# Behind the passes of a cross-attention: a reordered last pair of steps, head products in turns, fewer filler products, and one more wait for GpSimd

## What is computed

```python
x = x + xattn(ctx, layernorm(x), ...)     # 16 heads of 64, over 4096 context rows and the 256 rows
x = x + performer(layernorm(x), ...)      # linear attention, 16 heads of 16, 44 features each
x = x + moe(layernorm(x), ...)            # 8 experts, top 2, and a shared one

# the end of xattn, for each head
attn = softmax(sim);  out = attn @ v;  return out @ Wout + bout
# the end of performer
out = (context, qp, d_inv);  h = out @ Wo.T + bo;  return relu(h @ Wfc.T + bfc)
# moe, for each expert e (the shared one is the ninth)
hpre = x @ W1[e] + b1[e];  y = silu(hpre) @ W2[e] + b2[e]
```

## Time and profile before

| | |
|---|---|
| median of 3 runs | 664.42 us (664.26 to 666.61) |
| profiled execution | 664.24 us, of which the span of the trace is 662.5 us |
| PE busy | 649.3 us (98% of the span) |
| DVE, ACT, POOL busy | 508.8, 415.5, 277.0 us |
| granted TensorE clock | 1.0 throughout |
| attention ends, performer ends, last instruction | 514.5, 549.2, 662.5 us |

### The profile page before, as it was taken

The page is one execution under the profiler, slowest core; times in us unless marked ns, Lnnn a source line. Parts: engine busy times, 40 slices in busy tenths (PEclk is TensorE's granted clock), DMA queues, the critical chain, the costliest instruction groups (busy, mean ns, idle before and its releaser), DMA issues. The chain is left out here.

```text
span 662.5 us, 14524 instructions
## 1 busy us (share of the span) xinstructions
PE 649.3 (98%) x5202; PEld 523.5 (79%) x5202; DVE 508.8 (77%) x1010; ACT 415.5 (63%) x881; POOL 277.0 (42%) x210
## 2 busy tenths in 40 slices
PE   8899999999999999999999999999999999899998
PEld 7677777777777777777777777777776878899998
DVE  5899999876877777787777767877776676977674
ACT  5788889866665665665666665656664434655651
POOL 3656556444344354343444434434441300464640
PEclk9999999999999999999999999999999999999999
DMA  6201430010000010000000000000000302665500
GB/s 211 73 34 34 143 132 13 6 33 1 2 17 2 2 49 1 2 1 17 1 1 2 1 1 1 1 17 2 1 1 1 128 1 65 224 216 197 169 21 17
DMA packets 26164, 30.51 MB, mean 46 GB/s; under 512 B 4201, under 2 KB 23794, under 8 KB 26098
## 3 DMA queue, kind: packets, MB, share of 16 engines
q1 hardware_dynamic: 24594, 28.86, 13.2%
q10 hardware_dynamic: 1504, 0.79, 0.4%
HBM read 29.38 MB, written 0.26 MB: 45 GB/s over the span
## 5 line engine op out<-in xcount | busy, mean ns | idle before, releaser
L943 POOL TENSOR_TENSOR k_rms<-k_ss,neg_half 128x4 f32<-128x4 f32 x136 | 195.3, 1436 | 244.9 <-DVE k_ss L797 244.9
L624 ACT ACTIVATE probs<-s_ps,minus_bound 128x512 f32<-128x512 f32 x272 | 165.0, 689 | 103.6 <-PE s_ps L443 101.7
L169 PE MATMUL kv_ps<-w_quad,xn 128*128 128x512 f32 x816 | 206.8, 402 | 0.8 <-DVE xn L744 0.6
L791 DVE SCALAR_TENSOR_TENSOR probs_sum<-probs,tile_mask,probs_sum 128x512 f32<-128x512 f32 x264 | 191.1, 744 | 5.7 <-ACT probs L624 5.6
L169 PEld LDWEIGHTS kv_ps<-w_quad,xn 128*128 128x128 f32 x816 | 147.8, 188 | 39.1 <-DVE xn L744 0.8
L456 PE MATMUL o_ps<-probs,v 128*64 128x256 f32 x1088 | 132.6, 385 | 0.8 <-ACT probs L624 0.7
L443 PEld LDWEIGHTS s_ps<-q_parts,kt 64*128 64x128 f32 x1632 | 101.1, 185 | 26.2 <-issue 24.2
L443 PE MATMUL s_ps<-q_parts,kt 64*128 64x256 f32 x1632 | 114.9, 287 | 0.0
L456 PEld LDWEIGHTS o_ps<-probs,v 128*64 128x64 f32 x1088 | 72.0, 136 | 42.0 <-issue 10.9
L775 DVE SCALAR_TENSOR_TENSOR kn<-k_rms,kv_ps 128x256 f32<-128x256 f32 x136 | 56.4, 414 | 52.0 <-POOL k_rms L943 50.7
L616 ACT ACTIVATE kt<-s_ps 128x256 fp32r<-128x256 f32 x136 | 44.9, 382 | 45.3 <-PE s_ps L427 45.3
(11 more groups left out here) (212 smaller groups left out, 643.7 us busy)
## 6 DMA issues: line engine op xcount, KB each, us to landing
w_raw<-in_ffn_W SPq DMA_DIRECT2D x18, 1024.0 KB, 5.3
rows<-in_ctx SPq DMA_DIRECT2D x7, 512.0 KB, 3.9
w_raw<-in_L_xattn_Wkv SPq DMA_DIRECT2D x6, 256.0 KB, 3.3
wout<-in_L_xattn_Wout SPq DMA_DIRECT2D x4, 256.0 KB, 2.7
wq_raw<-in_L_xattn_Wq SPq DMA_DIRECT2D x3, 256.0 KB, 2.7
rows<-in_ctx SPq DMA_DIRECT2D x2, 256.0 KB, 5.1
w_raw<-in_L_xattn_Wkv ACTq DMA_DIRECT2D x2, 256.0 KB, 5.0
wq_raw<-in_L_xattn_Wq ACTq DMA_DIRECT2D x1, 256.0 KB, 3.9
```

Source lines behind the costliest of these rows:

```text
L169: last = nc.tensor.matmul(out, stationary(k, s), moving(k, m), start=n == 0, stop=n == len(terms) - 1)
L624: nc.scalar.activation(probs[n % P_RING][:, :, c, :], s_ps[n % 2][c][:], ACT.Exp, bias=minus_bound[:]).then_inc(exp_done, 1)
L791: nc.vector.scalar_tensor_tensor(total, probs[n % P_RING][:, :, c, :], seen, total, ALU.mult, ALU.add).then_inc(sum_done, 1)
L943: nc.gpsimd.tensor_tensor(k_rms[n % 2][:].rearrange("p i c -> p (i c)"), k_ss[n % 2][:].rearrange("p i c -> p (i c)"), neg_half[:, 0:4], A ...
```

## The change

Five edits, all behind or at the end of the passes.

1. In turn m = 67, PE makes the scores of steps 134 and 135 ahead of `weight_v(133)` instead of behind it; ACT copies the keys of 134 and 135 ahead of the exponentials of step 133, and DVE splits them ahead of the sums of step 133.
2. The totals and the head products come in turn: totals of pair 0, heads of pair 0, totals of pair 1, heads of pair 1. The totals of a pair get a bank of their own; DVE takes a reciprocal of four for each pair, and adds pair 0 before it waits for pair 1.
3. In the performer, the product with `feat_eps` waits for the first of two subtractions of keys (`k_shifted`) and not for both.
4. The bias products (`bfc`) move ahead of the products with `Wo`, into banks 0 and 7; of the fillers around them, 3 are gone, 3 have become 2, 1 is gone, and the last 3 have become 1.
5. GpSimd waits until VectorE has split both halves of expert 0's activations (`act_lo` at 2) before it enters its loop.

```diff
@@ attention, PE
-            def last_totals():
...
-                for i in range(QT):
-                    for j in range(2):
-                        for c in range(2):
-                            last = nc.tensor.matmul(totals_q[:, i, j, c:c + 1], probs_sum[g % 2][:, j, c, i * P:(i + 1) * P], ones[:, 0:1],
-                                                    start=True, stop=True, skip_group_check=True)
-                last.then_inc(totals_done, 1)
-            def last_heads():
                 pe.wait_ge(wout_in, 16 * NPASS)
                 for j in range(2):
+                    for i in range(QT):
+                        for c in range(2):
+                            last = nc.tensor.matmul(totals_q(j)[:, i, c:c + 1], probs_sum[g % 2][:, j, c, i * P:(i + 1) * P], ones[:, 0:1],
+                                                    start=True, stop=True, skip_group_check=True)
+                    last.then_inc(totals_done, 1)
                     pe.wait_ge(kept_done, NPASS + j)
...
                 for n in (e - 2, e - 1):
-                    if exists(n):
+                    if exists(n) and not (m == last_pair and n == e - 1):
                         weight_v(n)
...
                 for n in (e, e + 1):
                     if exists(n):
                         scores(n)
+                if m == last_pair:
+                    weight_v(e - 1)
@@ attention, ACT
                 for n in (e, e + 1):
                     if m and exists(n):
                         keep_kt(n)
+                if m == last_pair:
+                    weights(e - 1)
@@ attention, DVE
                 for j in range(2):
+                    dve.wait_ge(totals_done, NPASS + j)
+                    nc.vector.reciprocal(inverse_q[:, j], totals_q(j)).then_inc(inverse_done, 1)
+                    dve.wait_ge(inverse_done, 4 * (NPASS - 1) + j + 1)
                     dve.wait_ge(y_done, NPASS + j)
...
-                if exists(e - 2):
+                if exists(e - 2) and m != last_pair:
                     add_weights(e - 1, 0)
                 for n in (e, e + 1):
                     if m and exists(n):
                         kt_rest(n)
+                if m == last_pair:
+                    add_weights(e - 1, 0)
@@ performer, PE
-            pe.wait_ge(k_shifted, 2)
+            pe.wait_ge(k_shifted, 1)
...
-            busy(7, 3)
+            for j in range(QT):
+                nc.tensor.matmul(fc_ps(j), ones[0:1, :], spread["bfc"][0:1, :], start=True, stop=False)
             for k in range(KD):
                 pe.wait_ge(ot_kept, k + 1)
...
                 if k == 0:
-                    busy(7, 3)
-            for j in range(QT):
-                nc.tensor.matmul(ps[:, j, 0:D], ones[0:1, :], spread["bfc"][0:1, :], start=True, stop=False)
-            busy(7, 1)
+                    busy(3, 2)
             for k in range(KD):
                 pe.wait_ge(ht_kept, k + 1)
...
-            busy(7, 3)
+            busy(3, 1)
@@ experts, GpSimd
             biases(Turn(0, 2))
             biases(Turn(1, 2))
+
+            pool.wait_ge(act_lo, 2)
             run(pool, lo1, 2, E1, 2)
```

More of the change, by code:

```diff
@@ L1081, in exponents, with fc_ps @@
             return ps[:, b:b + 2, 0:EW].rearrange("p b (h m) -> p b h m", m=M)
+        def fc_ps(j):
+            return ps[:, 7 if j else 0, 0:D]
         def diagonal(n):
@@ L1212, in _ @@
                 for j in range(QT):
-                    last = nc.tensor.matmul(ps[:, j, 0:D], h_t[:, k, j * P:(j + 1) * P], w["Wfc"][:, k, :],
+                    last = nc.tensor.matmul(fc_ps(j), h_t[:, k, j * P:(j + 1) * P], w["Wfc"][:, k, :],
                                             start=False, stop=k == KD - 1)
@@ L1342, in _ @@
                 dve.wait_ge(fc_done, j + 1)
[L1343 removed]
+                last = nc.vector.scalar_tensor_tensor(x_res[:, j, :], fc_ps(j), 0.0, x_res[:, j, :], ALU.max, ALU.add)
             last.then_inc(own, 1)
```

16 lines of the change are left out of this document (7 added, 9 removed).

## The result

| | before | after |
|---|---|---|
| median of 7 runs, side by side | 666.10 us (664.26 to 666.61) | 660.67 us (658.93 to 662.12) |
| ratio after to before, from all executions (that of the two medians is 0.9918) | | 0.9927, 95% interval 0.9907 to 0.9948 |
| span of the profiled execution, its mean granted clock | 662.5 us, 1.0 | 658.9 us, 0.997 |

The kernel is 5.4 us faster by the medians. The forecast was 658.2 with a range up to 660.4; the measured 660.67 lies 0.27 us above that range. The seven executions after fall into groups by the mean clock that each was granted: spans of 657.2, 657.7 and 658.0 us at 1.00, 658.9 at 0.997, and 659.8, 660.3 and 660.4 at 0.995. That grouping turned out to be half of the story.

What follows compares the result with a forecast made beforehand. Bound by PE's products from 571.4 us on, and before that by hand-overs where fillers make PE look busy. 0.67 + 0.65 + 2.72 + 2.10 = 6.14 us off 664.24 gives 658.10, with 0.2 for the median 658.2; range 657.2 to 660.4.

Steps and rivals of the forecast that it cites:

- Last pair: Attention's last two steps: VectorE reaches the keys sooner, so the scores start earlier; gain 0.67 us, at worst 0.3.
- what follows keeps its distances: Behind the last pair's scores: everything later moves up by the same amount, so the 0.67 us is kept.
- Totals and heads in turn: Totals and head products: VectorE starts 0.93 us sooner and ends 0.65 sooner; gain 0.65 us, or 0.5.
- the products of pair 1 end when they did: Totals and heads: alternating them leaves PE's end for pair 1 unchanged; VectorE's second four adds run from 511.77 to 513.38.
- Performer: Performer block: `k_shifted` 0.40 us plus moved bias products and fewer fillers, together 2.72 us (2.0 to 2.9); barrier goes by VectorE.
- GpSimd's wait: Experts, turn 0: VectorE's second subtraction runs alone, so the second half of `down(0)` starts 2.10 us sooner.
- I take about 0.2 ... ahead of `lo2`: Experts: GpSimd is at work about 0.2 us after its wait, before `lo2` asks for the shared path at 0.35 to 0.4.
- the lower bound of my unknown, 0.07 us: Experts: least time for GpSimd's start after its wait, that of any hand-over; upper bound 0.53 us, a whole barrier.
- the two cases that I held apart at 0.4 us: Experts: GpSimd starting within 0.4 us of its wait goes ahead of `lo2`; starting later, `lo2` goes first.
- GpSimd comes too late: Rival, chance 0.20, experts: `lo2` goes first, GpSimd runs until 574.15, `up(2)` waits 0.8 us; 659.0 us.
- The collision a turn on: Experts, turn 1: GpSimd and VectorE's second subtraction nearly tie for the shared path; costs 0 to 0.2 us.
- The clock: Rival, chance 0.03: with fillers cut, TensorE's clock falls from 2.4 to 1.2 GHz into the experts; slower, up to 669.7 us.

Runs made afterwards that it cites:

- experiment 8: Totals of both pairs put ahead of all head products, on top of the changed kernel; 661.24 us.
- experiment 9: Totals of both pairs put ahead of all head products, on top of the changed kernel, a second time; 661.96 us.
- experiment 3: Changed kernel with GpSimd's subtraction of turn 2 written ahead of its loop, right behind the wait, so no branch stands between; 659.03 us median, ratio to before 0.9905.
- experiment 5: Changed kernel with GpSimd waiting for VectorE's cast only (`act_hi` at 2 in place of `act_lo` at 2); 658.33 us median, ratio to before 0.9910.
- experiment 2: Kernel before with GpSimd's wait alone added; 663.38 us median, ratio to before 0.9975.
- experiment 6: Changed kernel with more fillers kept at the performer's end (3 between the `Wo` products, 1 ahead of `Wfc`, 3 at the end); 660.87 us median, ratio 0.9945.
- experiment 4: Changed kernel with two filler products in PE's gap ahead of `up(2)`; 660.26 us median, ratio to before 0.9920.
- experiment 10: The kernel of experiment 5 (GpSimd waits for the cast only) run again; 659.42 us median, ratio to before 0.9910.
- experiment 11: The kernel of experiment 5 with four filler products in each of PE's two gaps at the start of attention; 658.39 us median, ratio to before 0.9905.
- experiment 12: The kernel of experiment 11, with both gaps at the start filled, a second time; 658.44 us median, ratio to before 0.9898.
- experiment 1: Changed kernel without GpSimd's new wait (edits 1 to 4 alone); 661.41 us median, ratio to before 0.9946.

## Why the prediction was right and where it failed

Two steps failed: the race for the path that GpSimd and VectorE share, which cost 0.8 us, and TensorE's clock, which the sum put at nothing and which fell in four of seven executions. A third, the totals, was sized 0.19 us too high.

**Last pair: the mechanism right, the number with a little luck.** 0.67 us forecast, 0.67 measured; the scores of step 135 do not wait, as worked out with 0.27 us of cover. But the scores came 0.77 us sooner, and "what follows keeps its distances" did not hold by the 0.10 in front of the first total.

**Totals and heads in turn: the mechanism right, the size 0.46 for 0.65.** VectorE starts 2.20 us behind the first total, against 3.13 before: 0.93, as forecast. The term mis-sized is "the products of pair 1 end when they did". In turn, the 32 records take PE 4.06 us (507.50 to 511.56) and not 3.78, so the second four head products start 0.18 us later than the sum had them. VectorE's last four adds start 0.13 later by that and take 1.66 us instead of 1.61, so they end 0.18 later. That the turning itself costs PE the 0.28 us is likely but not shown, since experiments 8 and 9 were lost to the clock.

**Performer: the mechanism right, the equal number luck.** 2.72 us forecast, 2.72 measured, and the barrier goes by VectorE. But the parts differ. VectorE's first row on the products with the features comes 22.07 us behind the performer's start instead of 22.70, so `k_shifted`, the only edit ahead of it there, gave 0.63 us and not the 0.40 of PE's idle time. Against that, `Wfc` follows `Wo` by 1.26 us (1.16 forecast), and VectorE's adds follow `Wfc` by 1.60 (1.50 forecast). The two errors cancel.

**GpSimd's wait: the step that failed is "I take about 0.2 ... ahead of `lo2`".** The size of the start was near: the recorded start came 0.25 us behind VectorE's subtraction. By the Trainium skill, "Advanced Engine Details and Errata", Control Flow Timing, an unconditional branch alone is about 51 ns; the chain of waits of after shows 0.26 us from the first piece on GpSimd's sequencer (563.72) to the subtraction (563.98), of which experiment 3 takes away 0.18 with the branch and what comes with it. What was wrong is the race. First, its other side was misread: `lo2` was put 0.35 to 0.4 us behind the end of the subtraction, as if it stood behind the whole of the small copy. Before, the subtraction ends at 571.32, and the timeline has `lo2` 0.26 us later:

```profile
571.58 2.27 DVE L1588 TENSOR_TENSOR e_w_second<-w_raw,e_w_second 128x2048 fp32r<-128x2048 f32 x1
```

In after it comes 0.25 us behind, in the same hundredth as GpSimd. Second, I compared a recorded start with the moment at which `lo2` asks for the path, and took the first start for the winner. Experiment 3 gives GpSimd a start 0.17 us ahead and it loses all the same. Even the lower bound of my unknown, 0.07 us, ends in the rival's case, so the two cases that I held apart at 0.4 us were never apart. The rival "GpSimd comes too late" had the rest right: `lo2` first, GpSimd until 570.67, `up(2)` waiting, here 0.77 us for the 0.8 forecast. It gave 659.0 us, and the undisturbed executions after are at 658.93, 659.49 and 659.68. Experiment 5, which repairs only this, lands within 0.3 us of the 6.14 of the sum (656.5 against 662.7 beside it, the middle of the undisturbed executions; 656.6 against 662.5 by the profiles).

**The collision a turn on** went as the near tie allowed: GpSimd first (572.87 against 573.12), VectorE's subtraction 5.51 us long, and no PE gap in `down(1)`. It cost nothing.

**The clock: a rival with 0.03 that held in part, and a term that the sum put at nothing.** It did not turn the sign, but it set the median, and it is what took the median out of the range. The forecast treated the clock as a property of the kernel, read from one execution in which PE was busy for 3.75 of 6 us at a granted 1.00. Over all executions of this study the kernel before fell in many: of 43 executions beside experiments, 21 had a mean of 1.00, 17 of 0.997, and 5 of 0.995. None with a fall was profiled, so where it fell is not shown; experiment 2, whose code is the same up to the experts, fell at 18 to 22 us, which begins inside the stretch of the earlier trace rows. The warning of the Trainium skill, "TensorE: Matmul & The Clock Gate", HAM oscillation, that waits between bursts of products let the next burst start slow, is borne out in kind by `up(2)` at 7.45 us, and not as a rule of every execution: in the profiles of experiments 2, 3, 6 and 8 the same 0.75 to 0.78 us gap stands in front of `up(2)`, in experiment 9 one of 1.79, and only in experiment 3 did the clock fall there. The gaps are far shorter than the waits of its example.

**The accounts close.** Profiled execution after: 656.4 by the sum, plus 0.19 (totals), 0.8 (gap), 1.53 (7.45 - 5.92) and 0.5 for the later start, less 0.4 in the experts that stays open (below), makes 659.0; the span is 658.9. And the median: the forecast put it 0.2 us above the profiled execution, from three runs of which two lay low. Four of seven runs after had at least one fall, so the median is one with a fall. The three without any are at 658.93, 659.49 and 659.68, inside the range.

**What stays open.** Why a gap brings a fall in one execution and not in the next. Whether the changed kernel falls more often than before in its new gap: executions with that gap (after, experiments 2, 3 and 6; 8 and 9, which fell at other places, left aside) have a mean of 0.995 in 6 of 28, the kernel before in 5 of 43, versions of the change without it in 2 of 25 (experiments 4, 5, 10 to 12) and, with the old stall in its place, in 2 of 6 (experiment 1); that points that way and proves little. And why, in the profiles of after and of experiment 1, the products with W1 of turns 3 and 4 take 5.61 us where before and experiment 5 have 5.81, while turns 5 and on have 5.61 in all four: 0.4 us in favour of after. No edit explains it: experiment 10, the same kernel as experiment 5, has 5.61 in both turns. It hides in the account of its experts' block (113.23 - 2.10 + 0.8 + 1.53 - 0.4 = 113.06, measured 112.98).

## What to carry to other kernels

A delay that is meant to put one engine ahead of another must leave the margin that the hand-over needs: release the slower starter one instruction *early*, so that it is already queued when the path comes free, and not exactly when it should go. It worked in all four profiles with that release. Where two operations share a path, read who kept its bare duration to see who went first, and not whose start is recorded first. And when a kernel's time moves by one or two microseconds from run to run, sort the executions by their granted clock before taking a median or a trace as *the* time: filling PE's waits where nothing is delayed by it went with 0.8 us in the median here (nine executions against eleven, not certain), while fillers behind the last consumer cost 0.6.

## What the runs showed of the hardware that was not expected

- A GpSimd subtraction whose recorded start lies 0.17 us ahead of VectorE's subtraction (564.58 and 564.75) still let VectorE go first; one that was already waiting when VectorE ended (562.29 against 563.31) went next. So it was in the first collision of thirteen of fourteen profiles; in one VectorE's cast of 0.68 us went in between.
- A blocked VectorE cast of 0.69 us is recorded with 4.97 us, and the blocked subtractions with 5.2 to 6.4: the whole wait stands inside the operation's own time.
- The granted clock fell to 0.50 for about 3 us behind idle times of PE as short as 0.77 us (`up(2)`), in the head products right behind the one-column totals with hardly a gap (510 to 514 us), and at the performer's end with PE recorded as busy (541 to 544), each in some executions of the same program only. One fall costs 1.4 us of span in the kernel before and 0.8 to 2.0 in the versions (middle of the executions at 0.997 against middle of those at 1.00).
- The same 32 records of one-column totals and head products took PE 4.06 us in four alternating groups and 3.78 in two.
